# Attention and routing of a post-norm layer: one product for output and router logits, second variance on ScalarE, routing by eight tiles

## The chip, the cores and the metric

One Trainium2 chip; the kernel runs on one of its cores. The metric is the time of one execution on the device in microseconds (us), the median of several runs; the kernel before took 134.73 us (three runs, 134.23 to 137.53).

## What is computed

x is 2 x 1024 tokens of 128 floats. Weights: Wqkv 128 x 384, Wout 128 x 128, a router of 14 experts, and per expert w1 128 x 256 and w2 256 x 128 with biases. gamma and beta are not trivial.

```
xn  = layer_norm(x) * gamma + beta
q, k, v = split(xn @ Wqkv) in 16 heads of 8;  q = elu(q) + 1;  k = elu(k) + 1
kv  = sum over l of k v^T (per batch and head);  out = (q @ kv) / (q . sum(k) + 1e-6)
x   = layernorm(x + (x + out @ Wout))                # no gamma, no beta
logits = x @ router_w;  a = argmax(logits);  weight = softmax(logits)[a]
y   = (gelu(x @ w1[a] + b1[a]) @ w2[a] + b2[a]) * weight
return layernorm(x + y)
```

Everything is float32. Attention is linear: no token looks at another except through the sums kv and sum(k).

## The kernel before

The five engines run hand-written programs side by side, tied by semaphores; each engine works strictly in the order in which its calls stand. 2048 tokens are 16 tiles (NT) of 128; four tiles are a chunk c (C = 4), chunks 0 and 1 are batch 0, chunks 2 and 3 batch 1.

First part, attention and routing. Per chunk: VectorE (DVE) takes statistics of x (stats1), GpSimd (POOL) a power of -0.5 (rstd_1) and the normalized tiles (norm1, L341; chunk 0 on DVE, L526). TensorE (PE) transposes them (tr_x), ScalarE (ACT) copies them out with gamma and beta (xt, L392). TensorE makes q transposed (proj_q) and k, v (proj_kv); ACT takes exp and relu of q and k and copies v (L397 to L404), DVE joins them to elu + 1 (elu_q L545, elu_k L551). sum_kv adds the key-value sums and, by a column of ones in v_sb, sum(k) for a batch; heads (L557, L560) masks them into heads. num multiplies q with them, divide (L565 to L570) divides by the denominator, the result is transposed again (tr_att, at L408), multiplied with Wout (proj_out), and DVE adds 2 x (pre, L578), takes its statistics (stats2_, L582 to L587), POOL the power (rstd_2), DVE normalizes (x1, L593). These rows are transposed once more (tr_x1, x1t L412) and multiplied with the router (logits).

Routing, per chunk of four tiles: route (L603 to L610) finds the first largest logit in four dependent steps; eexp (L416) and weigh (L615, L616) make the weight, the 129th column of a row; store_x1 (L278, on SP's queue) writes the chunk's rows to DRAM. ranks adds, with matrices of ones, how many tokens go before each token when sorted by expert. After the last chunk: place (L621 to L629) and sixteen at_spot (L632) turn the ranks into one-hot matrices, invert multiplies them to the list of source rows, steps (L637 to L640) and step_row (L693) give the list of (tile, expert) pairs.

Second part, experts. All sorted tiles are gathered from DRAM by POOL (L365), which waits for the four stores and for sources (L644). 29 steps j (NP) follow, one pair of tile and expert each: SP copies the expert's w1 (L283), PE turns the tile (L905) and multiplies it, ACT applies gelu (L452), PE multiplies with w2, DVE adds (L710); finished tiles are normalized and scattered by POOL (L378). Each engine loads the list of experts into registers first. The orders of all engines around this change are the plain lists of calls at the end of each engine's function.

Of the kernel before, what the change touches and what calls it, by code (L numbers as in the profile page):

```python
# [17 lines left out]
I32 = mybir.dt.int32  # L18
# [22 lines left out]
TE = NT + 1  # L41
GROUPS = [(0, 1), (1, 4), (4, 8), (8, 12), (12, 15), (15, 16)]
# [19 lines left out]
def build(nc, x, gamma, beta, wqkv, wout, router_w, w1, b1, w2, b2, out):  # L62
    with ExitStack() as ctx:
# [29 lines left out]
        wout_sb = sb("wout_sb", [P, D])  # L93
        rw_sb = sb("rw_sb", [P, E])
        vec_rows = sb("vec_rows", [E * FC + 2, P])
# [12 lines left out]
        stats2 = sb("stats2", [P, NT, 6])  # L108
        mv2 = sb("mv2", [P, NT, 2])
        ve = sb("ve", [P, NT])  # L110
        ve2 = sb("ve2", [P, NT])
        rstd = sb("rstd", [P, NT])
        shift = sb("shift", [P, NT])
        rstd2 = sb("rstd2", [P, NT])
        exponent = sb("exponent", [P, C])
        xn = sb("xn", [P, NT, D])
        xn_t = sb("xn_t", [P, NT, P])
# [6 lines left out]
        v_sb = sb("v_sb", [P, NT, D + 1])  # L124
        kv_h = sb("kv_h", [P, B, D + H])
        den = sb("den", [P, C, H])
        rden = sb("rden", [P, C, H])
        att = sb("att", [P, NT, D])
        att_t = sb("att_t", [P, NT, P])
        pre = sb("pre", [P, NT, D])  # L130
        rows = sb("rows", [P, NT, ROW])
        x1_t = sb("x1_t", [P, NT, P])
# [3 lines left out]
        is_top = sb("is_top", [P, C, E])  # L136
        ranked = sb("ranked", [P, C, E])
# [3 lines left out]
        below = sb("below", [P, NT, E])  # L141
        e_exp = sb("e_exp", [P, NT, E])
# [31 lines left out]
        ps_t = ps("ps_t", [P, C, P])  # L174
        ps_q = ps("ps_q", [P, C * P])
        ps_kv = ps("ps_kv", [P, C, 2 * D])
        ps_acc = ps("ps_acc", [P, 512])
        ps_num = ps("ps_num", [P, 2, 512])
        ps_o = ps("ps_o", [P, C, P])
        ps_kvh = ps_acc[:, 0:D + 1]  # L180
        ps_vec = ps_acc[:, 0:E * FC + 2]
        num_v = ps_num[:, :, 0:2 * (D + H)].rearrange("p b (i n) -> p b i n", i=2)


        def ps_lg(c):
# [113 lines left out]
        def _(pool):  # L299
# [20 lines left out]
            for b in range(B):  # L320
                t = pool.iota(token_i[:, b * JB:(b + 1) * JB], pattern=[[1, JB]], base=b * S, channel_multiplier=JB)
# [636 lines left out]
```

## Time and profile before

| what | value |
|---|---|
| median of 3 runs | 134.73 us (134.23 to 137.53) |
| the profiled execution | 135.24 us |
| its span in the trace | 133.4 us |
| busy: PE, DVE, POOL, ACT | 86.3, 69.2, 54.4, 48.3 us |
| mean granted clock of TensorE | 0.833 |

The span runs from the first to the last recorded instruction; the rest of the 135.24 us lies round it. Engine names: PE is TensorE's matmuls, PEld its weight loads, SPq and ACTq the queues that issue DMAs. A float32 product of one tile is two rows (two weight loads and two matmuls) in the trace. L12 is line 12 of the kernel. The granted clock is 1.00 at 2.4 GHz and 0.50 at 1.2 GHz; in the first 12 us the rows say 1.00 although products there take as long as they do later at 0.50 (two rows of 512 columns 1.92 us from 11.25, and 1.02 us from 15.51).

### The profile page before, as it was taken

The numbers are of one execution on the slowest core, as the hardware profiler recorded it, in microseconds if no ns is written. First come the engines' busy times: TensorE is split into PE (matmuls) and PEld (weight loads), VectorE is DVE, ScalarE is ACT, GpSimd is POOL, SyncE is SP. The second block draws the span as 40 slices with busy tenths as digits, with TensorE's granted clock in tenths as the row PEclk, the third lists the DMA queues.
The fourth block names the chain that finished last, engine by engine and source line by source line (L and its number), as shares of the span: only waits on it lengthen the run. The fifth ranks groups of instructions, "written<-read, shape, count | busy, mean of one in ns | idle before, by whom it ended". The sixth has DMA issues, their size and how long they took to land.

```text
span 133.4 us, 2086 instructions
## 1 busy us (share of the span) xinstructions
PE 86.3 (65%) x547; PEld 71.3 (53%) x547; DVE 69.2 (52%) x297; ACT 48.3 (36%) x128; POOL 54.4 (41%) x78
## 2 busy tenths in 40 slices
PE   0038998989558953486370399989999886743000
PEld 0025686859457942366240399868788685632000
DVE  0999433688873897642793011433445766635000
ACT  1222786149210210120400144555556476553200
POOL 6386820004210003300005775757104386768871
PEclk9999999999968999655555557999999999995555
DMA  4899950000001002002200643455432433301110
GB/s 144 251 325 347 292 149 0 0 0 5 0 0 55 24 0 79 0 0 84 82 0 0 202 115 98 131 137 135 142 112 92 140 119 101 104 20 39 39 59 20
DMA packets 9673, 12.15 MB, mean 91 GB/s; under 512 B 1426, under 2 KB 7230, under 8 KB 9662
## 3 DMA queue, kind: packets, MB, share of 16 engines
q1 hardware_dynamic: 8420, 9.69, 22.4%
q0 software_dynamic: 1024, 2.11, 6.5%
q10 hardware_dynamic: 218, 0.22, 0.6%
q8 instruction: 5, 0.08, 0.3%
q14 instruction: 6, 0.05, 0.1%
HBM read 6.07 MB, written 2.11 MB: 61 GB/s over the span
## 4 chain that ended last, share of the span: by engine, by line
PE 38%; DVE 23%; POOL 18%; issue 8%; ACT 5%; DMA 2%; DVEq 1%; POOLq 1%
PE ps_kv L744 14%; POOL out L378 10%; PE ps_num L744 9%; POOL rstd L327 5%; PE ps_acc L744 4%; PE ps_q L744 3%; DVE rows L593 2%; DMA acc<-x_rows,source 2%; ACT k_parts L457 2%; DVE at_spot L632 2%; PE ps_o L792 2%; DVE pre L578 2%; DVE att L570 2%; PE ps_t L807 2%; DVE acc L710 1%
## 5 line engine op out<-in xcount | busy, mean ns | idle before, releaser
L327 POOL TENSOR_TENSOR rstd<-ve,exponent 128x4 f32<-128x4 f32 (+2 forms) x14 | 14.0, 999 | 42.4 <-DVE ve L587 32.0
L365 POOL DMA_INDIRECT acc<-x_rows,source x16 | 16.3, 1020 | 23.0 <-DVE source L644 16.8
L744 PE MATMUL ps_kv<-xs_t,w_cur 128*128 (+1 forms) x116 | 21.7, 316 | 1.7 <-DMA w_cur<-w_sb 1.2
L744 PE MATMUL ps_num<-w_sb,hid 128*128 x116 | 20.1, 299 | 3.7 <-ACT hid L452 3.2
L710 DVE SCALAR_TENSOR_TENSOR acc<-ps_num,share,acc 128x128 f32 (+1 forms) x29 | 10.2, 351 | 23.1 <-PE ps_num L744 18.9
L744 PEld LDWEIGHTS ps_kv<-xs_t,w_cur 128*128 128x128 f32 x116 | 16.8, 209 | 5.6 <-issue 4.6
L452 ACT ACTIVATE hid<-ps_kv,w_cur 128x128 f32<-128x128 f32 x58 | 18.1, 364 | 4.3 <-PE ps_kv L744 4.3
L378 POOL DMA_INDIRECT out<-k_parts,source x16 | 16.0, 999 | 7.9 <-ACT k_parts L457 5.7
L744 PEld LDWEIGHTS ps_num<-w_sb,hid 128*128 128x128 f32 x116 | 16.5, 205 | 5.1 <-issue 4.9
L457 ACT ACTIVATE k_parts<-acc,shift,rstd 128x128 f32<-128x128 f32 x16 | 7.1, 486 | 9.1 <-DVE shift L717 9.1
L744 PE MATMUL ps_kv<-wqkv_sb,xn_t 128*128 128x256 f32 x32 | 8.1, 396 | 0.4 <-ACT v_sb L404 0.4
L744 PEld LDWEIGHTS ps_kv<-wqkv_sb,xn_t 128*128 128x128 f32 x32 | 6.3, 204 | 2.9 <-ACT v_sb L404 1.2
L408 ACT COPY att_t<-ps_o 128x512 f32<-128x512 f32 x4 | 2.3, 586 | 14.0 <-PE ps_o L792 14.0
L807 PE MATMUL ps_t<-ident,rows 128*128 128x128 f32 x16 | 3.8, 377 | 5.6 <-DVE rows L593 5.6
L412 ACT COPY x_t<-ps_t 128x512 f32<-128x512 f32 x4 | 2.3, 585 | 13.8 <-PE ps_t L807 13.8
L447 ACT COPY xs_t<-ps_t 128x128 f32<-128x128 f32 x8 | 2.1, 266 | 14.0 <-PE ps_t L905 14.0
L744 PE MATMUL ps_num<-b_k,ones 128*128 x29 | 6.6, 229 | 0.0
L751 PE MATMUL ps_t<-ident,xn 128*128 128x128 f32 x16 | 3.4, 353 | 4.8 <-DVE xn L526 3.6
L341 POOL TENSOR_SCALAR xn<-x_sb,rstd,shift 128x128 f32<-128x128 f32 x12 | 5.7, 487 | 1.8 <-DVE shift L519 1.8
L807 PEld LDWEIGHTS ps_t<-ident,rows 128*128 128x128 f32 x16 | 2.5, 194 | 6.0 <-DVE rows L593 5.9
L392 ACT ACTIVATE xn_t<-ps_t,vec_cols 128x512 f32<-128x512 f32 x4 | 3.2, 790 | 6.5 <-PE ps_t L751 6.5
L744 PE MATMUL ps_num<-kv_h,q_t 128*128 128x144 f32 x32 | 4.8, 293 | 1.1 <-DVE kv_h L560 1.1
(123 smaller groups left out, 159.2 us busy)
## 6 DMA issues: line engine op xcount, KB each, us to landing
w_cur<-w_sb SPq DMA_DIRECT2D x29, 129.0 KB, 2.6
w_sb<-L_ffn_w SPq DMA_DIRECT2D x1, 1792.0 KB, 10.1
x_rows<-rows SPq DMA_DIRECT2D x4, 258.0 KB, 2.0
x_sb<-L_attn_x SPq DMA_DIRECT2D x4, 256.0 KB, 4.2
acc<-x_rows,source POOLq DMA_INDIRECT x16, 2.8
out<-k_parts,source POOLq DMA_INDIRECT x16, 2.3
wqkv_sb<-L_attn_Wqkv ACTq DMA_DIRECT2D x1, 192.0 KB, 4.9
wout_sb<-L_attn_Wout SPq DMA_DIRECT2D x1, 64.0 KB, 5.1
```

Source lines behind the costliest of these rows:

```text
L327: pool.tensor_tensor(out_, in_, exponent[:, 0:in_.shape[1]], ALU.pow).then_inc(done, 1)
L341: pool.tensor_scalar(xn[:, t, :], x_sb[:, t, :], rstd[:, t:t + 1], shift[:, t:t + 1], ALU.mult, ALU.add).then_inc(xn_ok, 1)
L365: pool.indirect_dma_start(acc[:, t, :], None, x1_rows, bass.IndirectOffsetOnAxis(ap=source[:, t:t + 1], axis=0), bounds_check=last_token, ...
L378: pool.indirect_dma_start(out_rows, bass.IndirectOffsetOnAxis(ap=source[:, t:t + 1], axis=0), res[:, t, :], None, bounds_check=last_token, ...
L392: act.activation(xn_t[:, C * c:C * c + C, :], ps_t[:], ACT.Identity, bias=vec_cols[:, E * FC + 1:E * FC + 2], scale=vec_cols[:, E * FC:E * ...
L452: act.activation(hid[:, k, c, :], ps_h[j % 2][:, c, :], ACT.Gelu, bias=w1_cur[:, k, F + c:F + c + 1]).then_inc(hid_ok, 1)
L457: act.activation(res[:, t, :], acc[:, t, 0:D], ACT.Identity, bias=shift3[:, t:t + 1], scale=rstd3[:, t:t + 1]).then_inc(y_ok, 1)
L570: dve.tensor_tensor(att[:, t:t + 2, :].rearrange("p i (h e) -> p i h e", e=HD), num_v[:, b, :, 0:D].rearrange("p i (h e) -> p i h e", e=HD ...
L710: dve.scalar_tensor_tensor(out=tile, in0=ps_y[j % 2], scalar=share[:].rearrange("p t e -> p (t e)")[:, bass.ds(tile_of(j, e) * E + e[j], 1 ...
L744: return pe.matmul(o, l, r, start=start, stop=stop)
L751: last = pe.transpose(ps_t[:, i, :], xn[:, C * c + i, :], ident[:])
L807: last = pe.transpose(ps_t[:, i, :], rows[:, C * c + i, 0:D], ident[:])
```

## The change

Output and logits from one product. The layer norm before the router takes off a mean and scales; both commute with the router's product. So Wout is multiplied on chip with [C | C Wr], where C = I - 1/128 centres and Wr is the router: cen_r, wo_t and wo_r (router_centre, weights_turn, weights_router, router_centred, router_out). The sums are now taken as v^T k (kv_t) and sum(k) in its own product with a column of ones (ps_ks), masked (own_heads) and multiplied with wo_r (values_out) into m_sb, 142 columns per batch. The queries are divided: den makes the denominators (epsilon comes in by a small product, den_eps), denominators takes the reciprocal, widen repeats it for the eight lanes of a head on ACT, turn_den transposes it, divide multiplies the transposed q. attend is then the one product; attended splits it into lg and pre (already centred up to 2 x). The part of the logits that comes from x itself is a product of the untouched transposed tiles (xh, residual) scaled by std (logits_x).

The second variance: squares on ACT, with the accumulated sum as output; POOL adds epsilon, takes the power and a shift (rstd_2); x1 is an ACT piece too. Logits are compared unscaled; soften scales them for the exponential once rstd2 is there.

Routing runs over eight tiles (p = 0, 1) instead of four (c = 0 to 3): route, eexp, weigh, ranks. Constants and the split of b2 move from DVE's head and middle: the iotas and the split to POOL behind norm1, the casts to DVE's middle. keep_busy adds products of zeros on TensorE (240 columns, bfloat16) at the start, behind the last attend, ranks(1) and invert, and ahead of the experts.

```diff
+            def residual(c):
+                for i in range(C):
+                    last = mm(res_of(c)[:, i, :], xh_t[:, C * c + i, :], cen_r[:, D:DL])
...
+                for t in range(C * c, C * c + C):
+                    mm(ps_kvt, v_sb[:, t, :], k_sb[:, t, :], False, False)
+                    last = mm(ps_ks, k_sb[:, t, :], one_col[:], False, t % JB == JB - 1)
...
+                mm(ps_m, kv_t[:, b, :], wo_r[:]).then_inc(m_ps, 1)
...
+                for i in range(C):
+                    last = mm(den_c[:, H * i:H * i + H], q_t[:, C * c + i, :], ks_h[:, c // CB, :], False, i == C - 1)
...
+                    last = pe.transpose(r_of(c)[:, i * P:i * P + P], q_exp[:, (C * c + i) * P:(C * c + i + 1) * P], ident[:])
...
+                for i in range(C):
+                    last = mm(ps_o[:, i, 0:DL], qs_t[:, C * c + i, :], m_sb[:, c // CB, :])
...
+            def squares(c):
+                act.wait_ge(pre_ok, c + 1)
+                act.wait_ge(neg2m_ok, 2)
+                for t in range(C * c, C * c + C):
+                    act.activation(rows[:, t, 0:D], pre[:, t, :], ACT.Square, bias=neg2m_s[:, t:t + 1], scale=ROOT_D,
+                                   accum_out=var2[:, t:t + 1]).then_inc(var2_ok, 1)
+            def x1(c):
+                act.wait_ge(shift2_ok, c + 1)
+                for t in range(C * c, C * c + C):
+                    act.activation(rows[:, t, 0:D], pre[:, t, :], ACT.Identity, bias=shift2[:, t:t + 1],
+                                   scale=rstd2[:, t:t + 1]).then_inc(x1_ok, 1)
...
+            def soften(p):
+                dve.wait_ge(rstd2_ok, CB * p + CB)
+                dve.tensor_tensor(scaled[:, o, :], below[:, o, :], rstd2[:, o].unsqueeze(2).to_broadcast([P, PT, E]),
+                                  ALU.mult).then_inc(below_ok, 1)
...
             def store_x1(c):
-                sp.wait_ge(x1_ok, c + 1)
-                sp.wait_ge(weight_ok, c + 1)
+                sp.wait_ge(x1_ok, C * c + C)
+                sp.wait_ge(weight_ok, c // CB + 1)
```

The lines of a diff are cut here; the order of TensorE's calls from the first sum on is now: sum_kv(1), residual(0), residual(1), values_out(0), den(0), den(1), proj_kv(2), residual(2), turn_den(0), residual(3), turn_den(1), proj_q(2), sum_kv(2), attend(0), proj_kv(3), attend(1), proj_q(3), sum_kv(3), values_out(1), den(2), den(3), ranks(0), turn_den(2), turn_den(3), attend(2), attend(3), 10 fillers, ranks(1), 14 fillers, invert, 4 fillers. DVE's from there: own_heads(0), elu_q(1), denominators(0), logits_x(0), logits_x(1), denominators(1), divide(0), logits_x(2), logits_x(3), divide(1), elu_k(2), constants, attended(0), elu_q(2), elu_k(3), attended(1), own_heads(1), elu_q(3), denominators(2), denominators(3), route(0), divide(2), divide(3), attended(2), attended(3), soften(0), route(1), place.

DVE between the one-hot matrices and the step list, before:

```order
L632 TENSOR_SCALAR at_spot<-col_no,spot 128x128 x16
L637 CAST begin_i<-ps_acc 128x14
L638 TENSOR_SCALAR btile_i<-begin_i 128x14 [waits dve_s]
L639 TENSOR_TENSOR begun<-btile_i,step_e 128x13 [waits dve_s]
L640 TENSOR_REDUCE count<-begun 128x1 [waits dve_s]
L644 CAST source<-ps_o 128x16 [waits src_ps]
L693 CAST step_row<-ps_t 1x32 [waits row_ps]
```

And after the change:

```order
L733 TENSOR_SCALAR at_spot<-col_no,spot 128x128 x16
L738 CAST begin_i<-ps_k 128x14
L739 TENSOR_SCALAR btile_i<-begin_i 128x14 [waits dve_s]
L740 TENSOR_TENSOR begun<-btile_i,step_e 128x13 [waits dve_s]
L741 TENSOR_REDUCE count<-begun 128x1 [waits dve_s]
L716 TENSOR_REDUCE e_sum<-e_exp 128x8 [waits eexp_ok]
L717 RECIPROCAL rows<-e_sum 128x8 [waits dve_s]
L710 TENSOR_TENSOR scaled<-below,rstd 128x112 [waits rstd2_ok]
L745 CAST source<-ps_a 128x16 [waits src_ps]
L716 TENSOR_REDUCE e_sum<-e_exp 128x8 [waits eexp_ok]
L717 RECIPROCAL rows<-e_sum 128x8 [waits dve_s]
L801 CAST step_row<-ps_t 1x32 [waits row_ps]
```

weigh(0), soften(1) (L710) and weigh(1) now stand round sources, behind at_spot; before, all weights were made ahead of place.

ACT's last work ahead of the Gelu table load, before:

```order
L408 COPY att_t<-ps_o 128x512 [waits at_ps]
L416 ACTIVATE e_exp<-below 128x56 [waits below_ok]
L408 COPY att_t<-ps_o 128x512 [waits at_ps]
L412 COPY x_t<-ps_t 128x512 [waits x1t_ps] x2
L416 ACTIVATE e_exp<-below 128x56 [waits below_ok] x2
L460 ACT_TABLE_LOAD
```

And after the change:

```order
L505 ACTIVATE rows,var<-pre,neg2m_s 128x128 [waits neg2m_ok,pre_ok]
L505 ACTIVATE rows,var<-pre,neg2m_s 128x128 x3
L511 ACTIVATE e_exp<-scaled 128x112 [waits below_ok]
L516 ACTIVATE rows<-pre,shift,rstd 128x128 [waits shift2_ok]
L516 ACTIVATE rows<-pre,shift,rstd 128x128 x3
L511 ACTIVATE e_exp<-scaled 128x112 [waits below_ok]
L516 ACTIVATE rows<-pre,shift,rstd 128x128 [waits shift2_ok]
L516 ACTIVATE rows<-pre,shift,rstd 128x128 x3
L516 ACTIVATE rows<-pre,shift,rstd 128x128 [waits shift2_ok]
L516 ACTIVATE rows<-pre,shift,rstd 128x128 x3
L574 ACT_TABLE_LOAD
```

The x1 pieces (L516) of chunks 2 and 3 stand behind the second e_exp; before, x1 was DVE's and stood ahead of its routing.

## Rows read from the trace of the kernel before

**Rows 1.** Stretches: width; busy PE, PEld, DVE, ACT, POOL; granted clock; DMA, GB/s
```profile
60.00:70.00 10.00, 5.95 (x39) 4.45 (x36) 6.64 (x35) 1.53 (x2) 0.00 (x0) 0.50 0.15 55
...
76.00:80.00 4.00, 4.00 (x19) 3.91 (x20) 0.39 (x2) 1.68 (x6) 3.09 (x4) 0.50 0.51 140
80.00:90.00 10.00, 9.50 (x68) 8.10 (x67) 3.25 (x13) 5.21 (x21) 6.46 (x7) 0.90 0.48 125
```

**Rows 2.** Timeline, handover from routing to experts: start us, us, instruction, [idle before <-releaser]
```profile
66.91 2.68 DVE L632 TENSOR_SCALAR at_spot<-col_no,spot 128x128 bf16<-128x128 bf16 x16
...
71.28 1.42 POOL L365 DMA_INDIRECT acc<-x_rows,source  x1 [16.80 <-DVE source L644]
73.00 1.00 POOL L365 DMA_INDIRECT acc<-x_rows,source  x1 [0.30 <-issue]
```

**Rows 3.** Timeline, start of the experts; last the store's DMA issues (KB, us to landing)
```profile
70.21 0.17 DVE L644 CAST source<-ps_o 128x16 int32<-128x16 f32 x1
...
73.16 6.68 SPq L283 DMA_DIRECT2D w_cur<-w_sb  x6
...
74.41 0.45 PE L905 MATMUL ps_t<-ident,acc 128*128 128x128 f32 x1 [3.80 <-DMA acc<-x_rows,source]
...
76.19 2.02 PE L744 MATMUL ps_kv<-xs_t,w_cur 128*128 128x128 f32 x8
...
x_rows<-rows SPq DMA_DIRECT2D x4, 258.0 KB, 2.0
```

**Rows 4.** Timeline, TensorE's products and transposes of four tiles
```profile
22.57 1.25 PE L744 MATMUL ps_num<-kv_h,q_t 128*128 128x144 f32 x8 [0.60 <-DVE kv_h L560]
...
29.99 1.89 PE L744 MATMUL ps_kv<-wqkv_sb,xn_t 128*128 128x256 f32 x8
...
32.61 1.06 PE L744 MATMUL ps_acc<-v_sb,k_sb 128*128 128x129 f32 x8
...
33.58 0.66 PE L807 MATMUL ps_t<-ident,rows 128*128 128x128 f32 x4
...
34.96 1.03 PE L744 MATMUL ps_q<-rw_sb,x_t 128*128 128x14 f32 x8 [0.72 <-issue]
...
55.97 1.89 PE L744 MATMUL ps_q<-rw_sb,x_t 128*128 128x14 f32 x8 [0.68 <-ACT x_t L412]
```

**Rows 5.** Timeline and groups by form: pieces of ACT, DVE and POOL
```profile
8.50 1.79 POOL L341 TENSOR_SCALAR xn<-x_sb,rstd,shift 128x128 f32<-128x128 f32 x4 [0.39 <-DVE shift L519]
...
19.42 0.59 ACT L403 ACTIVATE k_parts<-ps_kv 128x512 f32<-128x512 f32 x1
...
19.89 0.59 ACT L404 COPY v_sb<-ps_kv 128x512 f32<-128x512 f32 x1
...
51.13 0.69 DVE L578 SCALAR_TENSOR_TENSOR pre<-x_sb,ps_o 128x512 f32<-128x512 f32 x1 [0.80 <-PE ps_o L744]
...
53.25 1.11 DVE L593 TENSOR_SCALAR rows<-pre,mv,rstd 128x128 f32<-128x128 f32 x4
...
58.40 0.22 DVE L605 TENSOR_TENSOR ranked<-is_top,prio 128x56 f32<-128x56 f32 x1
...
64.97 0.39 DVE L621 TENSOR_TENSOR place_m<-ps_acc,chosen 128x224 f32<-128x224 f32 x1 [0.41 <-PE ps_acc L744]
...
122.59 1.26 ACT L457 ACTIVATE k_parts<-acc,shift,rstd 128x128 f32<-128x128 f32 x3 [2.07 <-DVE shift L717]
...
125.69 0.49 ACT L457 ACTIVATE k_parts<-acc,shift,rstd 128x128 f32<-128x128 f32 x1 [1.83 <-DVE shift L717]
...
L327 POOL TENSOR_TENSOR rstd<-ve,exponent 128x4 f32<-128x4 f32 x8 | 9.0, 1119 | 34.6 <-DVE ve L587 32.0 <-DVE ve L513 2.6
...
L567 DVE RECIPROCAL rden<-den 128x64 f32<-128x64 f32 x4 | 2.2, 553 | 0.1
```

**Rows 6.** Stretches of one us where the clock falls, columns as in rows 1
```profile
36.00:37.00 1.00, 0.00 (x0) 0.00 (x0) 0.23 (x1) 0.00 (x0) 1.00 (x1) 1.00 0.00 0
...
38.00:39.00 1.00, 0.69 (x3) 0.70 (x4) 0.90 (x5) 0.00 (x0) 0.00 (x0) 0.50 0.00 0
```

More of the change, by code:

```diff
@@ new lines, in eexp @@
+            def eexp(p):
+                o = slice(PT * p, PT * p + PT)
+                act.wait_ge(below_ok, p + 1)
+                act.activation(e_exp[:, o, :], scaled[:, o, :], ACT.Exp).then_inc(eexp_ok, 1)
+            def x1(c):
[3 more added lines that the diff above has]
+                                   scale=rstd2[:, t:t + 1]).then_inc(x1_ok, 1)
@@ L433, in _ @@
-            kv(3)
-            x1t(0)
-            x1t(1)
+            xh(3)
+            heads_out(0)
+            widen(0)
+            widen(1)
+            k(2)
+            v(2)
+            q(2)
+            k(3)
+            v(3)
+            q(3)
+            heads_out(1)
+            widen(2)
+            widen(3)
+            squares(0)
+            squares(1)
+            x1(0)
+            squares(2)
+            squares(3)
             eexp(0)
-            at(2)
+            x1(1)
@@ L843, in invert, with keep_busy @@
                 last.then_inc(src_ps, 1)
+            def keep_busy(bank, n):
+                for i in range(n):
+                    mm(bank, ones[:], nothing[:])
+            idle_k = ps_k[:, 2, 0:240]
+            idle_q = ps_q[:, 0:240]
+            pe.wait_ge(filler_ok, 2)
+            keep_busy(idle_k, 16)
             pe.wait_ge(pool_c, P_IDENT)
@@ L875, in _ @@
-            logits(0)
-            tr_x1(1)
+            sum_kv(1)
+            residual(0)
+            residual(1)
+            values_out(0)
+            den(0)
+            den(1)
+            proj_kv(2)
+            residual(2)
+            turn_den(0)
+            residual(3)
+            turn_den(1)
+            proj_q(2)
+            sum_kv(2)
+            attend(0)
+            proj_kv(3)
+            attend(1)
+            proj_q(3)
             sum_kv(3)
-            num(2)
-            pe.wait_ge(pool_c, P_ONES)
@@ L880, in _ @@
-            pe.wait_ge(consts_ok, N_CONSTS)
+            values_out(1)
+            den(2)
+            den(3)
             ranks(0)
-            logits(1)
-            tr_att(2)
-            num(3)
-            proj_out(2)
-            ranks(1)
-            tr_att(3)
-            proj_out(3)
-            tr_x1(2)
-            logits(2)
-            tr_x1(3)
-            ranks(2)
-            logits(3)
-            ranks(3)
+            turn_den(2)
+            turn_den(3)
+            attend(2)
```

641 lines of the change are left out of this document (361 added, 280 removed).

## The prediction

> About 2% (2.7 us) is what a measurement of this kernel can tell from no change.
>
> **What bounds it now.** I read the stretches first. From 60 to 70 us TensorE is busy for 5.95 of 10 us at a granted clock of 0.50, its 1.2 GHz level, and it is still there from 76 to 80; the mean of 0.90 from 80 to 90 puts the rise at 82 [rows 1]. So there are two parts. Until about 70 us each engine waits for another in turn and none is full. After the routing the experts run on TensorE, and at the end POOL's queue of scatters. Then the handover between the two: the sixteen at_spot end at 69.59, POOL begins the first gather at 71.28 and takes 1.3 for each further one [rows 2]; the source indices leave DVE at 70.38, TensorE turns the first gathered tile at 74.41 and has the first expert from 76.19 [rows 3], 6.6 us behind at_spot. Nothing behind that point is edited except for filler products, so the change pays as far as this start comes earlier, or the clock there is higher.
>
> **Durations.** In float32 a product of four tiles with 14 columns takes 1.03 us at full clock and 1.89 at half [rows 4]: only the weight loads count, 0.24 a tile at full clock. With 256 columns it takes 1.89, with 144 columns 1.25, with 129 columns 1.06, and four transposes 0.66 [rows 4]. Some 0.16 to 0.2 of each is the way out of the array, which the next product covers, so they occupy TensorE for 1.71, 0.96, 0.9 and 0.43. Two ACT pieces of 512 columns begin 0.5 apart, a reciprocal of 64 takes 0.55, an element-wise DVE step of 512 takes 0.69 [rows 5]. A link of the routing chain is 0.22 us at 56 elements [rows 5]; at DVE's 0.69 for 512, 56 more add 0.07, so 0.3 at 112 with its wait.
>
> **The first part, laid out with these.** It ends at 69.6 now. After the change:
> 1. The constants leave DVE's head and the shift before the second normalization goes, so POOL's norm(1), at 8.50 now [rows 5], begins about 7.7 and takes 1.8. With TensorE kept warm by 32 filler products, one set of transposes 0.43 and the first key/value product 1.9 bring it to 11.8. Cold it would be about 2 more.
> 2. ACT's exp, relu, v and the new copy xh, 4 x 0.5, let tr_x(2) go at 14.0; 0.43 and 1.9: the second key/value product ends at 16.3.
> 3. ACT again, 3.1 us for k(1), v(1), xh(1), q(0); then q(1) 0.85 and transposes 0.43 on TensorE. sum_kv now loads two sets of weights a tile, 8 x 0.24 = 1.9 against 0.9: 22.7. Here the kernel stands at 22.57 now, with its first num product [rows 4]: the xh copies and the longer sums have eaten the early lead.
> 4. TensorE in its order: residual 4 x 0.94, values_out 0.24, den 2 x 1.0, key/value(2) 1.71, turn_den 2 x 0.43, q(2) 0.85. That is 9.4, to 32.1.
> 5. elu_k(2) stands behind divide(1): 0.7; sum_kv(2) 1.9; attend(0) 0.95; key/value(3) 1.7; ACT 1.1; elu_k(3) 0.7; sum_kv(3) 2.0; masks 0.5; den(2), den(3) 2.4; reciprocal 0.6; 0.5 for handovers: 44.6 + 0.5 = 45.1.
> 6. route(0) over eight tiles 4 x 0.3 + 0.5 = 1.7; ranks(0), 3304 columns at 2.4 GHz, 1.4; a turn 0.6; divide 0.7; attend(2) 1.1; lg and pre 0.9; attend(3) 1.1; lg and pre 0.9; 0.3 for handovers: 53.8. soften(0) 0.3, route(1) 1.7, ranks(1) 1.2; place from place_m to at_spot 1.95 and at_spot 2.65 as now [rows 2, 5]: 61.7.
>
> That is 7.9 us before the 69.6 of now. Gone are the transposes of att and x1, their copies, proj_out and the logits as products of their own, of which the last rounds ran at half clock, two of four routing chains, and the statistics of pre on DVE. The same layout made for the kernel of now comes to 71.1, so it is more likely long than short where the clock is high.
>
> **What it gives back.** The rows of the two orders show a new chain. The x1 pieces of chunks 2 and 3 stand on ACT behind eexp(1), which needs soften(1), and that stands on DVE behind at_spot, steps and weigh(0). POOL gathers only when all four stores have landed. From 61.7: steps 0.8, weigh(0) 0.5, soften(1) 0.3, eexp 0.35, then eight x1 pieces. One ACT piece of this form takes 0.49 and three take 1.26 [rows 5], so 0.39 each: 3.2, to 66.9. The last store needs 2.0 from issue to landing [rows 3]: 69.0; POOL's 0.9, as between 70.38 and 71.28: the first gather at 69.9. Now x1 is long done and the gather stands 1.7 behind at_spot; then 8.2. Of 7.9 us, 6.5 are given back. With the distances of now turn(0) comes 3.1 later, at 73.0, and the first expert at 74.8 instead of 76.2: 1.4 earlier. SP's first weight copy, issued at 73.16 [rows 3], 2.8 behind the sources, now stands behind the last store: 67.3 + 2.8 = 70.1. That is 4.7 ahead of the first expert, 3.0 before: hidden. weigh(1), behind sources, is done by 64.2, under x1. Behind the x1 pieces on ACT is only the Gelu table load, which ends before turn(0).
>
> DVE does four x1 pieces in 1.11 us [rows 5], 0.26 each with its tail off, where ACT needs 0.39. The Trainium skill, "ScalarE: Activation LUTs" (Rules for kernel authors), puts plain multiplies and adds on VectorE and not on ScalarE, and so speaks against this move; by it the eight late pieces would take 2.1 instead of 3.2. The trace agrees on which engine is faster, though in float32 by a factor of 1.5 only. The sum goes by the order as written, 3.2.
>
> Operations without a row. Squares with an accumulated output: from 0.26 (DVE's piece) to 0.8 (an ACT piece and as much again for the read-out), I take 0.4; chunk 3's squares and POOL's power (mean 1.12 [rows 5]) end by 57, soften(1) asks at 63.0, so a cover of 6 us makes both ends cost nothing. The widening copy: 0.4 to 1.0, taken as 0.5 by the copies of 512; from den(3) to turn_den(2) it is partly hidden by route(0), so 0 to 0.5 more. Products with one column: 0.24 a tile by the row with 14 columns, bounds 0.12 and 0.3; sixteen on the path, -2 to +1. The split of b2 and the constants on POOL lie in its idle time between 17 and 47.
>
> **The clock.** TensorE had nothing to do from 36 to 37 at a granted clock of 1.00, and had 0.50 from 38 to 39 [rows 6]. After the change idle stretches of 2.5 us (44.4 to 46.9) and 2.1 us (53.8 to 55.9) remain; a short fall in one of them costs about 0.5, which I add. At the experts' start the clock is 0.50 from 76.2 to 82 now [rows 1]: at full clock that work takes 2.9 less, of which the gathers, 1.3 apart [rows 2], let perhaps 2.2 through. 24 fillers now run from about 66.7 and 6 between the first turns, but 3 to 4 us without work lie between. Held warm it is -2.2, cold 0; I take 1.1.
>
> The Trainium skill, "TensorE: Matmul & The Clock Gate" (HAM oscillation), warns that waits between bursts put the array back to half rate. If that acts between these fillers and turn(0), this term is 0 and the sum 1.1 higher; the fall at 38 shows that it can.
>
> Sum: span 133.4 - 1.4 - 1.1 + 0.5 = 131.4. The profiled execution took 135.24, 1.84 round its span, so 133.2 after; it stands 0.5 above the median of 134.73, which gives 132.7.
>
> **Rivals.**
> A. The clock holds: fillers carry it to the experts, no gap drops it, and the layout is a microsecond long as it was for now: 133.4 - 1.4 - 2.2 - 1.0 = 128.8, by the median 130.1. For it: fillers stand ahead of every late wait. Against: the gap ahead of turn(0).
> B. Slower: the clock falls while ranks(0) waits for route(0) and stays at half until the routing is done, as it does from 55 to 70 now. The products from 47 to 57 double (ranks, turns, attend): +3.3, and the experts start cold: 133.4 - 1.4 + 3.3 = 135.3, by the median 136.6. It decides from where at_spot ends later than 63.1, since only 1.4 are left after the give-back. With the fall at 42, under den, it is +6.9: 140.2.
> C. The late stores are no wait, something lets x1(3) go early: 7.9 and the clock's 1.1 come through, 125.7. The orders of DVE and ACT speak against it.
>
> Forecast 0.45, A 0.27, C 0.03, B 0.25. Faster by over 2% (under 132.0): A, C and a sixth of the forecast, 0.37. Slower by over 2% (over 137.4): the heavy part of B, 0.15. Within: 0.48. Range 129.3 to 137.0.
>
> **What would show it.** At_spot ends between 60 and 63; eexp(1), eight ACT pieces of 0.39 and the last store lie between it and the first gather, which begins 8 us behind it; the first expert at 74.8. The granted clock at 77 tells A from the rest. It is wrong if the gather stands less than 6 us behind at_spot, or at_spot ends after 64.

## The result, and the profile after

The changed kernel took 142.64 us in the median of four runs (140.84 to 145.81) beside 136.13 (134.23 to 137.78) of the kernel before: ratio 1.052, 95% interval 1.041 to 1.064. It is slower; the prediction was 132.7, range 129.3 to 137.0. Every kernel also has executions some per cent slower than its fastest, so each ratio here is taken between the faster executions of both kernels, while the times given are medians of all. The profiled execution is the 145.81 one, 3 us above the median, with the lowest mean clock of the four (0.821); so its times are read for where the excess lies, and the median for how large it is. Its span is 144.1 us.

The stretches of the changed kernel. Columns as in rows 1; the last three rows answer to those of [rows 1]:

```profile
20.00:30.00 10.00, 8.90 (x64) 8.25 (x64) 2.54 (x5) 6.63 (x13) 5.31 (x20) 0.89 0.02 4
30.00:40.00 10.00, 10.00 (x42) 9.29 (x43) 2.12 (x6) 2.80 (x5) 0.00 (x0) 0.50 0.00 1
40.00:50.00 10.00, 10.00 (x42) 8.58 (x42) 3.57 (x13) 1.08 (x2) 0.00 (x0) 0.59 0.00 0
...
60.00:70.00 10.00, 8.21 (x51) 6.91 (x51) 3.92 (x12) 6.22 (x29) 3.87 (x8) 0.74 0.00 1
...
76.00:80.00 4.00, 2.31 (x17) 1.28 (x16) 3.52 (x22) 1.30 (x4) 0.00 (x0) 0.87 0.14 51
80.00:90.00 10.00, 5.76 (x37) 4.26 (x37) 0.54 (x2) 4.03 (x10) 4.38 (x5) 0.71 0.49 158
```

From 30 to 40 us TensorE has work in every microsecond and a granted clock of 0.50, its 1.2 GHz level. In [rows 1] the low clock went with 5.95 busy us of ten; from 76 to 80 us TensorE was busy throughout at 0.50 there too, but the clock had been low since 55 us, behind three microseconds (51 to 54) almost without work. Here it falls under work. Single microseconds of the same trace show the fall:

```profile
26.00:27.00 1.00, 1.00 (x12) 1.00 (x11) 0.61 (x3) 0.50 (x2) 0.00 (x0) 1.00 0.00 0
27.00:28.00 1.00, 1.00 (x10) 1.00 (x10) 0.42 (x1) 0.00 (x0) 0.00 (x0) 0.87 0.02 4
28.00:29.00 1.00, 1.00 (x6) 0.92 (x6) 0.00 (x0) 0.00 (x0) 0.00 (x0) 0.50 0.03 5
```

What TensorE does there, in the timeline: the sixteen records of residual(0) and (1), two dens of four tiles, then the key/value product of four tiles that takes 3.76 us instead of the 1.89 of [rows 4].

```profile
26.21 2.19 PE L852 MATMUL ps_o<-cen_r,xh_t 128*128 128x14 f32 x16
...
28.93 1.87 PE L852 MATMUL ps_r<-ks_h,q_t 128*128 128x16 f32 x8
...
32.37 3.76 PE L852 MATMUL ps_k<-wqkv_sb,xn_t 128*128 128x256 f32 x8
```

At the start, the product of router weights waits for its load, six fillers stand behind it, and only then come the first transposes. These run at half speed, and the first key/value product does for a part (1.06 us for four transposes, 2.55 for the product; 0.63 and 1.89 later on), although 28 fillers had gone before the first transposes:

```profile
8.47 0.58 PE L852 MATMUL ps_o<-rw_sb,cen_r 128*128 128x14 f32 x2 [2.25 <-DMA rw_sb<-L_ffn_router_w]
8.89 1.36 PE L852 MATMUL ps_k<-nothing,ones 128*128 128x240 bf16 x6
10.04 1.06 PE L863 MATMUL ps_t<-ident,xn 128*128 128x128 f32 x4
...
12.76 2.55 PE L852 MATMUL ps_k<-wqkv_sb,xn_t 128*128 128x256 f32 x8
```

The chain of waits of the same kernel goes through POOL: its pieces, its small constants, and only then the first key/value sum (ps_a).

```profile
7.82 3.14 POOL xn L360 x4
...
16.48 3.68 POOL xn L360 x4
...
20.92 0.03 POOL one_col L406
20.95 0.15 POOL before L407
21.10 2.04 PE ps_a L852 x17
```

And the handover, in the timelines of DVE, ACT, POOL and TensorE, which answers to [rows 2, 3]:

```profile
74.73 2.69 DVE L733 TENSOR_SCALAR at_spot<-col_no,spot 128x128 bf16<-128x128 bf16 x16
...
78.90 3.17 ACT L516 ACTIVATE rows<-pre,shift,rstd 128x128 f32<-128x128 f32 x8
...
84.41 1.30 POOL L430 DMA_INDIRECT acc<-x_rows,source  x1 [11.44 <-DMA x_rows<-rows]
...
89.20 0.62 PE L852 MATMUL ps_q<-xs_t,w_cur 128*128 128x128 f32 x4
```

At_spot ends at 77.4 (69.6 before, 61.7 predicted). The first gather stands 7.0 behind it (1.7 before), the first expert 4.8 behind the gather, and the last scatter begins 51.0 us behind the first expert (140.15 - 89.20) where it was 53.4.

### The profile page after: what moved, and what is told of

It is laid out like the page before. It is cut to its first block, busy times and chain, and to the rows that moved or that the text cites. A ratio compares the mean times of both kernels' runs of the same rounds, so it can differ in the third digit from the quotient of the medians.

```text
span 144.1 us, 2336 instructions
## 1 busy us (share of the span) xinstructions
PE 108.0 (75%) x666; PEld 90.1 (63%) x666; DVE 54.9 (38%) x224; ACT 61.4 (43%) x178; POOL 64.8 (45%) x99
## 4 chain that ended last, share of the span: by engine, by line
PE 43%; POOL 22%; DVE 14%; issue 6%; DMA 5%; ACT 5%; DVEq 1%; POOLq 1%
PE ps_o L852 12%; PE ps_k L852 10%; POOL out L443 9%; PE ps_a L852 7%; POOL xn L360 7%; PE ps_q L852 6%; POOL rstd L349 5%; PE ps_t L852 2%; PE ps_r L852 2%; ACT rows L516 2%; DMA acc<-x_rows,source 2%; DMA x_sb<-L_attn_x 2%; ACT k_parts L571 2%; DVE at_spot L733 2%; DMA x_rows<-rows 1%
## 5 line engine op out<-in xcount | busy, mean ns | idle before, releaser
L852 PE MATMUL ps_o<-w_sb,hid 128*128 x116 | 19.2, 290 | 3.4 <-ACT hid L566 3.4
L852 PEld LDWEIGHTS ps_o<-w_sb,hid 128*128 128x128 f32 x116 | 15.6, 196 | 4.4 <-issue 4.1
L818 DVE SCALAR_TENSOR_TENSOR acc<-ps_o,share,acc 128x128 f32 (+1 forms) x29 | 10.2, 351 | 21.0 <-PE ps_o L852 14.3
L852 PE MATMUL ps_q<-xs_t,w_cur 128*128 (+1 forms) x60 | 10.4, 297 | 1.7 <-DMA w_cur<-w_sb 1.4
L566 ACT ACTIVATE hid<-ps_q,w_cur 128x128 f32<-128x128 f32 x30 | 9.3, 364 | 2.4 <-PE ps_q L852 2.4
L360 POOL TENSOR_SCALAR xn<-x_sb,mv,rstd 128x128 f32<-128x128 f32 x12 | 9.9, 839 | 0.6 <-POOL rstd L349 0.6
L852 PE MATMUL ps_k<-wqkv_sb,xn_t 128*128 128x256 f32 x32 | 10.2, 475 | 0.0
L852 PE MATMUL ps_k<-xs_t,w_cur 128*128 x56 | 9.8, 297 | 0.4
L566 ACT ACTIVATE hid<-ps_k,w_cur 128x128 f32<-128x128 f32 x28 | 8.7, 365 | 1.7 <-PE ps_k L852 1.7
L852 PE MATMUL ps_a<-k_sb,v_sb 128*128 128x128 f32 x32 | 8.4, 357 | 0.1
L483 ACT ACTIVATE k_parts<-ps_k 128x512 f32<-128x512 f32 x4 | 2.4, 597 | 12.7 <-PE ps_k L852 12.7
```

The source lines that it names most:

```text
L360: pool.tensor_scalar(xn[:, t, :], x_sb[:, t, :], mv[:, t, 0:1], rstd[:, t:t + 1], ALU.subtract, ALU.mult).then_inc(xn_ok, 1)
L483: act.activation(k_exp[:, o, :], ps_k[:, :, 0:D], ACT.Exp).then_inc(k_act, 1)
L566: act.activation(hid[:, k, c, :], ps_h[j % 2][:, c, :], ACT.Gelu, bias=w1_cur[:, k, F + c:F + c + 1]).then_inc(hid_ok, 1)
L818: dve.scalar_tensor_tensor(out=tile, in0=ps_y[j % 2], scalar=share[:].rearrange("p t e -> p (t e)")[:, bass.ds(tile_of(j, e) * E + e[j], 1 ...
L852: return pe.matmul(o, l, r, start=start, stop=stop)
```

## The experiments

Sixteen kernels ran in four groups of four, each group on a chip of its own, so a time is compared only with the kernel before of its own group. In the first group (n_shift, n_contig, s_order, c_wide) that took 140.79 us, 4 to 6 more than in the others, and in all four traces ACT waits once for 2.4 to 3.5 us, 2 to 4 us behind the first expert, for something that the profile doesn't name; from the first gather to the last scatter they need 62.6 to 64.2 us, where all other traces need 55.7 to 58.4. No run tried why. These four are therefore read up to the first gather.

**1 and 2. POOL's pieces.** n_shift:

```diff
-  pool.tensor_scalar(xn[t], x_sb[t], mv[t, 0], rstd[t], ALU.subtract, ALU.mult)
+  pool.tensor_scalar(xn[t], x_sb[t], rstd[t], shift[t], ALU.mult, ALU.add)   # shift = -mean * rstd on DVE
```

> The changed kernel with one edit: POOL's norm1 in the form of before, x times rstd plus shift, the shift again made by DVE. Theory: the new form (x minus mean, times rstd) is what took POOL 3.12 us for four pieces instead of 1.79, and three such chunks stand on the path of the start (rows 7.82, 12.16, 16.48). Then four pieces take 1.8 again, sum_kv(0) begins at about 17 instead of 21.1, and the time falls by about 4 us to 138 or 139. Rival: POOL is slow because of what DVE or the DMAs do beside it, then four pieces stay at 3 us and the time stays at 142 to 143.

n_contig keeps subtract and mult, but takes the mean from a dense copy:

```diff
+  dve.tensor_copy(mean[chunk], mv[chunk, 0])
-  pool.tensor_scalar(xn[t], x_sb[t], mv[t, 0], rstd[t], ALU.subtract, ALU.mult)
+  pool.tensor_scalar(xn[t], x_sb[t], mean[t], rstd[t], ALU.subtract, ALU.mult)
```

> The changed kernel, norm1 still subtract then multiply, but the mean is read from a tile of its own, one number beside the next (a DVE copy), instead of every second number of mv. If the pair of operations is what POOL is slow at, four pieces stay at 3.1 us. If it is the place of the mean, they go back to 1.8 us.

n_shift took 151.51 us (147.12 to 152.43) beside 140.79, where 138 or 139 was expected, and n_contig 149.98 in its one run; no run tells why n_shift is this slow at its end. The dense mean left a piece at 0.79 us; multiply and add brought it to 0.45, as in the timeline of n_shift (four pieces):

```profile
8.27 1.74 POOL L361 TENSOR_SCALAR xn<-x_sb,rstd,shift 128x128 f32<-128x128 f32 x4 [0.38 <-DVE shift L643]
```

So the pair of operations sets the price. The sums of chunk 0 began at 18.9 instead of 21.1. The first batch's sums, DVE's kv_t(0), came at 27.4 us: no earlier than the 26.5 of the changed kernel's first trace, but that trace had no fall of the clock near 22 us, and n_shift has one. Its neighbours on the same chip, which have it too and keep the dear pieces (n_contig and s_order), come at 29.7 and 29.6. So the price was worth some 2 us there, by way of the column of ones behind the pieces (run 15), and 0.9 to 1.3 us at the end of at_spot (73.8, beside 74.7 and 75.1).

**3. Order of the handover.** s_order:

```diff
 ACT:  x1(1)  -eexp(1)  x1(2)  x1(3)  +eexp(1)
 DVE:  place  -at_spot  -steps  weigh(0)  soften(1)  +at_spot  +weigh(1)  +steps  sources  -weigh(1)
```

(at_spot is the end of place in the changed kernel.)

> The changed kernel with another order alone: on ACT x1(2) and x1(3) ahead of eexp(1); on DVE weigh(0) and soften(1) between the ids and the at_spot, weigh(1) ahead of steps and sources. Theory of the late stores: the first gather then begins 2 to 3 us behind the last at_spot instead of 7.0, though at_spot itself comes up to 1 us later; the time falls by 4 us. Rival: the experts' start is set by something else (SP's weight copies, register loads, fillers), then it falls by less than 1.5 us.

145.42 us, ratio 1.017 (1.001 to 1.034). Its ACT and POOL timelines:

```profile
68.43 4.71 ACT L516 ACTIVATE rows<-pre,shift,rstd 128x128 f32<-128x128 f32 x12
73.05 0.28 ACT L511 ACTIVATE e_exp<-scaled 128x112 f32<-128x112 f32 x1
...
78.62 1.30 POOL L430 DMA_INDIRECT acc<-x_rows,source  x1 [8.50 <-DMA x_rows<-rows]
```

The x1 pieces now lie under the search for the places. The gather stands 3.5 behind at_spot instead of 7.0 (2 to 3 was expected). The give-back of the prediction existed, and half of it was only order.

**4, 5 and 6. Wide products among the narrow ones.** A filler is a bf16 product of 240 columns, as the changed kernel has them elsewhere. c_wide:

```diff
 residual, den:  for i in range(C):
                     mm(14 or 16 columns)
+                    mm(filler)
```

> The changed kernel with one product of zeros of 240 columns behind each tile of residual and den (32 more in all, 0.1 us each at full clock). Theory: the granted clock falls to 0.50 at 28 and at 55 us, with TensorE busy all the time, because the products there have 14 or 16 columns and do little but load weights; with wide products among them it stays at 1.00, the stretch from 26 to 48 us shrinks by 6 to 9 us less 1.6 for the new products, and the time falls by 4 to 7 us. Rival: the clock falls for another reason (its own time grid, the load of earlier work), then the record is as before and the time grows by 1.6 to 3 us.

c_block sets the same fillers as four in a row ahead of each group of four; c_res has them in the residual alone.

> The changed kernel with the same 32 filler products of 240 columns as in the run that set one behind each narrow product, but in blocks of four ahead of each residual and each den, so that the narrow products still stand four in a row. Theory (the clock falls under runs of products that stream few columns for the time they occupy TensorE, and one wide product between two of them prevents it): the fall near 28 us comes again or only some us later, and most of 30 to 45 us is at 0.50. Rival (any extra wide products in that stretch hold the clock): 1.00 from 20 to 50 us, as with the interleaved ones, and at_spot ends at 66 to 68 us.

> The changed kernel with a wide filler behind each narrow product of the residual alone; den stays as it is (14 or 16 columns, four in a row). Theory: nothing falls at 28 us, since the residual's products no longer stand alone; den(0) and den(1) follow at 29 to 32 us and are the next narrow run, so the fall comes there, 2 to 5 us later, and at_spot ends between 67 and 76 us. Rival (the residual alone is the cause): 1.00 until 50 us, at_spot at 67 us.

Stretches of c_wide, of c_block and of c_res, in this order:

```profile
20.00:30.00 10.00, 9.22 (x87) 8.61 (x88) 3.15 (x8) 6.33 (x14) 4.99 (x19) 1.00 0.02 4
30.00:40.00 10.00, 9.54 (x77) 8.49 (x76) 4.01 (x17) 3.86 (x7) 0.00 (x0) 1.00 0.00 1
```

```profile
20.00:30.00 10.00, 8.93 (x62) 7.75 (x62) 2.53 (x5) 5.38 (x11) 4.81 (x18) 0.83 0.01 4
30.00:40.00 10.00, 9.54 (x76) 8.36 (x77) 3.91 (x14) 3.79 (x8) 0.00 (x0) 1.00 0.00 1
```

```profile
20.00:30.00 10.00, 9.03 (x41) 7.89 (x42) 0.92 (x3) 4.72 (x9) 4.40 (x19) 0.60 0.02 4
30.00:40.00 10.00, 10.00 (x50) 9.47 (x50) 2.25 (x7) 1.51 (x3) 0.00 (x0) 0.50 0.00 0
```

At_spot ends at 66.8 in c_wide, 71.6 in c_block, 78.2 in c_res. In c_block the rival was right as far as the clock goes: it had a short fall from 22 to 25, before the residual, and then held to 53, so four narrow products in a row did no harm here with four wide ones ahead of them; at_spot came later than the rival's 66 to 68. In c_res neither came: its clock fell at 22 us, before the residual, behind 2.7 us without work, and did not rise until 42, although the residual had its fillers by then. So there are two falls. The one at 28 stands alone in the changed kernel's first trace, and c_wide is its control: both wait 1.19 us ahead of the first sums, neither falls at 22, and with the fillers step 4 of the prediction takes 9.9 us (25.9 to 35.8) instead of 16.4. c_wide took 144.46 us, ratio 1.034 (1.021 to 1.047), where 4 to 7 us less was expected: of the 8 us by which its at_spot is earlier than n_contig's and s_order's on the same chip (10.6 earlier than in the first trace) the end shows little, on the chip with the unnamed wait. c_block took 140.62 us and c_res 147.28, one run each, beside 135.76.

**7, 8 and 9. Controls on another chip.** The changed kernel and the kernel before, unedited; and b_sub, the kernel before with the changed kernel's pair of operations:

```diff
-  pool.tensor_scalar(xn[t], x_sb[t], rstd[t], shift[t], ALU.mult, ALU.add)
+  pool.tensor_scalar(xn[t], x_sb[t], mv[t, 0], rstd[t], ALU.subtract, ALU.mult)
```

> The changed kernel, unedited, run beside the next three on one chip so that they can be compared with it. Theory (two mis-sized terms: POOL's pieces at 0.79 us instead of 0.45, and the clock at half under the narrow products): as in the first profile, the second set of key/value sums starts near 21 us, the clock is 0.50 for most of 30 to 45 us with TensorE busy throughout, at_spot ends at 75 to 78 us and the first gather stands 7 us behind it. Ratio to the kernel before 1.04 to 1.07. Rival (the chip of the first runs was the cause): at_spot ends before 70 us here and the ratio is under 1.03. The wait of 2.4 to 3.5 us of ACT for an unseen releaser behind the first expert, which the four variants so far all show and the first profile of the changed kernel does not: if it comes from the edits it is absent here, if it comes from the execution it can be here too.

> The kernel before, unedited, with a profile taken on the same chip. Theory: at_spot ends near 69.6 us and the first gather begins near 71.3 us, as in the first profile; if there is more in its time than then, it lies behind the first gather (until the last scatter 58.3 us then), as ACT's wait of 2.4 to 3.5 us and a lower clock. Rival: this chip is slower in the part up to the routing, so that at_spot ends after 72 us.

> The kernel before with one edit: POOL's twelve normalized tiles as (x - mean) * rstd, the form of the changed kernel, in place of x * rstd + shift. Theory (the pair of operations sets the price): one piece takes 0.79 us instead of 0.45, a chunk 3.1 us instead of 1.8, the three chunks +4 us in sum, and at_spot ends 2 to 4 us later, since chunks 1 to 3 gate the key/value products in turn. Rival (the price comes from what else runs beside it in the changed kernel, ACT's or DVE's traffic): the pieces keep 0.45 us.

The changed kernel: 140.74 us beside 135.12, ratio 1.038 (1.029 to 1.046), at_spot to 76.4, gather 7.0 behind, no unnamed wait. Its clock falls at 22 us, behind a wait of 2.68 us for the column of ones, rises at 29 and falls again at 32.4, with work in every microsecond, to 46. The kernel before (137.15 us in this run): at_spot to 72.1, 2.5 later than in its first trace (its mean clock from 40 to 50 us was 0.69), and 57.7 us from the first gather to the last scatter; so its excess over the first trace lies ahead of the gather, as the rival had it, and one trace against another carries some 2 us of this kind. B_sub's first chunk on POOL:

```profile
8.51 3.22 POOL L341 TENSOR_SCALAR xn<-x_sb,mv,rstd 128x128 f32<-128x128 f32 x4 [0.39 <-DVE shift L519]
```

0.80 a piece: the price is the pair's alone, as the theory had it. Its first sums come 1.3 us late and the second batch's 1.4 us late, yet at_spot ends at 71.7, no later than in the unedited kernel of this chip, and the time is 137.48 us beside its 137.15 (one run each). 2 to 4 us was expected; 1.4 came and was lost again, where the unedited kernel's clock was low for longer (39 to 46 us; b_sub's 40 to 43).

**10. Three repairs at once.** all3 is n_shift, s_order and c_wide together.

> The changed kernel with all three repairs: the normalization as x * rstd + shift (POOL 0.45 us a piece), eexp(1) and the late x1 pieces set ahead of at_spot, steps and sources, and a wide filler product of 240 columns behind each narrow one of the residual and of den. Theory (the three causes add): POOL's part takes 3 to 4 us from at_spot, the clock 8 to 10 us, so at_spot ends at 62 to 66 us and the first gather stands 3.5 us behind it, at 66 to 69 us, against 71.3 in the kernel before: ratio 0.95 to 0.99. Rival (the give-back moves on: the experts then begin cold or wait for weights): the first gather is as early but the time is within 1% of the kernel before.

134.12 us beside 135.12, ratio 0.997 (0.993 to 1.000): 4.7% under the unedited changed kernel's 140.74 on the same chip. At_spot ends at 66.8, as in c_wide, though the pieces are cheap here (its clock falls from 22 to 25 us, c_wide's did not). The gather stands 3.5 behind it, at 70.3. Expected were 62 to 66, 66 to 69 and a ratio of 0.95 to 0.99; what came is nearer to the rival. Two stretches offer a reason. The 24 fillers ahead of turn(0):

```profile
71.35 4.96 PE L865 MATMUL ps_q<-nothing,ones 128*128 128x240 bf16 x24 [3.13 <-issue]
```

run at half clock and hold the first gathered tile, issued at 70.3, until 76.1; in the changed kernel they began at 82.95, ahead of the first gather, and its 3 us covered most of them. And at the start:

```profile
8.20 0.38 PE L865 MATMUL ps_o<-rw_sb,cen_r 128*128 128x14 f32 x2 [1.96 <-DMA rw_sb<-L_ffn_router_w]
...
9.57 1.06 PE L876 MATMUL ps_t<-ident,xn 128*128 128x128 f32 x4
```

the product of router weights waits for its load, with six fillers behind it, ahead of the first transposes, whose input is ready at 7.5.

**11 and 12. Those two.** all3_rc sets the router product behind the first transposes; all4 has 4 fillers instead of 24 as well.

```diff
-  router_centre(); keep_busy(6); tr_x(0)
+  keep_busy(6); tr_x(0); router_centre()
...
-  keep_busy(idle_q, 24)
+  keep_busy(idle_q, 4)
```

> The kernel with the three repairs, with a fourth: the product of router weights, which waits for its load until 8.2 to 8.5 us, and the six fillers behind it no longer stand ahead of the first transposes in TensorE's order; the product comes behind them. Theory (this wait, which the prediction left out, is most of the 2.2 us by which the first key/value product ends late): the first transposes begin near 7.6 us instead of 9.6, the first key/value product ends at 12 to 12.5 instead of 14, at_spot ends 1 to 2 us earlier than the 66.8 of three repairs; ratio 0.98 to 0.99 to the kernel before. Rival (ACT's exits or POOL's pieces bind right behind it): kv_t(0) moves by less than 0.5 us and the ratio stays at 0.997.

> The same with a fifth edit: 4 fillers instead of 24 ahead of the first gathered tile's turn. In the run with three repairs these 24 ran at half clock, 4.96 us from 71.35, and held turn(0) until 76.3 us, though the first gathered tile had landed near 74. Theory: turn(0) begins when its tile lands, 4 us behind the first gather, so the first expert starts about 2 us earlier than in the run before this; of that 1 to 2 us reach the end, ratio 0.965 to 0.985. Rival (the fillers pay for themselves in clock: without them the experts begin at half clock, as in the kernel before): the first expert is earlier, the clock is 0.50 for its first 4 to 6 us and the ratio is that of the run before this or worse.

134.86 us (130.61 to 135.03) and 132.71 (129.26 to 134.81) beside 135.76; no interval, and the two overlap. In all3_rc the first key/value product ends at 12.3 instead of 13.8, but kv_t(0) comes at 27.8 and at_spot ends at 67.8, each a microsecond later than in all3, where 1 to 2 earlier was expected: TensorE was done earlier, then waited 2.14 us for the column of ones, and its clock was at 0.50 from 20 to 26 (in all3 from 22 to 25). The clock ate the lead. In all4 the first expert begins at 76.5, 1.8 earlier than in all3_rc, as expected, at half clock for its first microsecond.

**13 and 14. Narrowness by itself.** In the kernel before, behind the first batch's sums, where TensorE waits for nothing:

```diff
+  b_narrow: for i in range(32): mm(unused, xn_t[i % 4], wqkv_sb[:, 0:14])
+  b_broad:  for i in range(16): mm(unused, xn_t[i % 4], wqkv_sb[:, 128:384])
```

> The kernel before with 32 float32 products of 14 columns (what the residual and den are made of) set on TensorE behind the first batch's key/value sum, where its granted clock is 1.00 and it waits for nothing; their results are not used. Each occupies 0.24 us, 7.7 us in all, with TensorE busy throughout. Theory (a run of narrow products is itself enough to lower the clock): it falls to 0.50 within or right behind the block, between 25 and 32 us, although TensorE is busy 1.00 of each us; later steps move by 8 us or more. Rival (the falls come from idle stretches alone): the clock stays 1.00 through the block, as long as TensorE is busy.

> The control to the run before: the same place and the same 7.5 us, filled with 16 float32 products of 256 columns, 0.47 us each. Both theories: the clock stays at 1.00 through the block. If it falls here too, it is not the narrowness but the length of the busy stretch, and the theory of the narrow products is wrong.

Stretches of b_narrow, then of b_broad:

```profile
26.00:27.00 1.00, 1.00 (x11) 1.00 (x11) 0.00 (x0) 0.00 (x0) 0.00 (x0) 1.00 0.00 0
27.00:28.00 1.00, 1.00 (x8) 1.00 (x7) 0.00 (x0) 0.00 (x0) 0.00 (x0) 0.64 0.00 0
28.00:29.00 1.00, 1.00 (x7) 1.00 (x6) 0.00 (x0) 0.00 (x0) 0.00 (x0) 0.50 0.00 0
```

```profile
26.00:27.00 1.00, 1.00 (x6) 0.87 (x6) 0.00 (x0) 0.00 (x0) 0.00 (x0) 1.00 0.00 0
27.00:28.00 1.00, 1.00 (x7) 0.87 (x6) 0.00 (x0) 0.00 (x0) 0.00 (x0) 1.00 0.00 0
28.00:29.00 1.00, 1.00 (x6) 0.90 (x5) 0.00 (x0) 0.00 (x0) 0.00 (x0) 1.00 0.06 16
```

Both are busy in every microsecond of their blocks (21.8 to 30.2 and 23.0 to 30.0). Under the narrow products the clock falls at 27.3, stays at 0.50 behind them to 34, and the 1.89 us product there takes 2.79; under the broad ones it never moves. So narrow products are enough for a fall, without a wait. The times do not tell the two apart: 143.56 us for b_narrow, 145.61 for b_broad, one run each beside 137.04, since b_broad's clock falls later, at 43 us in a wait, and stays low to 57. And one thing is left of the changed kernel's own fall: in its first trace only 1.5 us of the residual had gone by, with the sums ahead of it (per tile one product of 128 columns and one of a single column). c_wide left these as they were and held; how much they add, no run parts.

**15. The column of ones.** a_one writes it ahead of POOL's normalizations:

```diff
+  pool.memset(one_col[:], 1.0)
   norm1(1); norm1(2); norm1(3); spreads()
-  pool.memset(one_col[:], 1.0)
```

> The changed kernel with the column of ones that the key/value sums multiply by written on POOL before its normalizations, not behind them; nothing else. In the changed kernel TensorE waits at 19.9 to 21.1 us for POOL's row of constants behind the twelve pieces. Theory (the sums wait for this column, not for the pieces of their own chunk, so that it, and not the pieces' price, is what gives the late first part): the sums of chunk 0 run at 18 us while ACT reads chunk 1, q(1) begins near 21 and kv_t(0) comes at 24 to 26 us instead of 26.5 to 30; the idle stretch before q(1) stays, so the clock still falls once near 20 and again under the narrow products; time 0 to 2% below the unedited changed kernel. Rival (the pieces of chunk 2 and 3 bind): kv_t(0) moves by less than 0.5 us.

140.65 us, ratio 1.047 (1.035 to 1.059), no gain that can be told. The sums of chunk 0 now run at 18.3 instead of 21.1. But q(1) waits for ACT as before:

```profile
21.64 1.45 PE L852 MATMUL ps_q<-xn_t,wqkv_sb 128*128 128x512 f32 x2 [1.44 <-ACT q_pos L478]
```

and the clock falls at 22 behind that gap, so kv_t(0) comes at 26.7 (24 to 26 was expected): earlier than in the second trace of the unedited kernel (29.9), not than in the first (26.5), where no fall came at 22. ACT sets q(1) in the first trace as well: it begins 3.23 us behind the second key/value product there, here and in all6. So the column by itself cost nothing in the first trace; in the second it made the wait of 2.68 us, behind which the clock fell. This trace, of a 140.28 us execution, shows the second fall too:

```profile
28.00:29.00 1.00, 1.00 (x11) 0.98 (x10) 0.00 (x0) 0.28 (x1) 0.00 (x0) 1.00 0.02 4
29.00:30.00 1.00, 1.00 (x8) 1.00 (x8) 0.09 (x1) 0.00 (x0) 0.00 (x0) 0.54 0.00 0
30.00:35.00 5.00, 5.00 (x17) 4.28 (x18) 1.21 (x4) 1.23 (x2) 0.00 (x0) 0.50 0.00 0
```

**16. All of it.** all6 is all4 with a_one's edit and with 12 fillers behind the sums of chunk 0.

```diff
   sum_kv(0)
+  keep_busy(a free bank, 12)
   proj_q(1)
```

> The kernel with the five edits (normalization as multiply and add, x1 ahead of at_spot, wide fillers between the narrow products, router product behind the first transposes, 4 fillers at the experts), and with the column of ones early and 12 wide fillers behind the sums of chunk 0, where TensorE idled and the clock fell to 0.50 from 19.8 to 26.7 us. Theory: 1.00 from 10 to 50 us, kv_t(0) at 23 to 24.5 us instead of 27.8 to 28.1, at_spot ends 3 to 4 us earlier than the 68 of then, at 64 to 65; ratio 0.94 to 0.965 to the kernel before. Rival (DVE or the late stores take it back): the first gather moves by less than 2 us from 71.6 us.

130.92 us (130.66 to 132.47) beside 137.04, ratio 0.976 (0.963 to 0.988), above the expected 0.94 to 0.965: it is faster than the kernel before, though whether by over 2% is not clear, and a_one, the changed kernel but for one column, took 140.65 on the same chip. The clock is 1.00 from 10 to 48 us, kv_t(0) comes at 24.0, at_spot ends at 65.5, the gather begins at 69.05. Two falls are left: one from 65 to 75 us, round the handover, and one in front of ranks(0), behind 2.1 us without work (stretch of all6):

```profile
48.00:50.00 2.00, 1.76 (x11) 1.51 (x12) 0.33 (x2) 2.00 (x12) 1.03 (x2) 0.53 0.01 4
```

## Why the prediction was wrong, by its steps

**Steps 1 to 3 (22.7 us): measured 26.4, +3.7.** Of this, 3.3 us are there at once: the first key/value product ends at 15.1, not 11.8. The prediction left out the wait for the router's weights and took TensorE as "kept warm by 32 filler products", where the first transposes and a part of this product ran at half speed. In all6, with the router product behind the transposes, the ones early and the gap filled, the product ends at 12.6 and the sums at 23.7, one microsecond from the forecast. The piece on POOL was mis-sized as well (a chunk 3.1, not 1.8). It delays the column of ones, which the prediction put among the constants that "lie in its idle time": one of them had a reader. That cost nothing in the first trace and a fall of the clock in the second.

**Step 4 ("that is 9.4, to 32.1"): measured 16.4, from 26.4 to 42.7, +6.9.** This is the step that failed. Each term was taken at full clock from [rows 4], and the clock was questioned only where TensorE would idle. It fell with the engine full, under products of 14 to 16 columns, as it does in b_narrow under nothing but such products, and what followed took twice as long. With fillers among them the step takes 9.9, in c_wide (25.9 to 35.8) and in all6 (23.7 to 33.6).

**Steps 5 and 6 (29.6 us): measured 34.7, +5.1.** The same low clock to 48, and again from 55, begun under den(2), to 65, the wait of ranks(0) included. In all3, where the clock stays at 1.00 until 66 us, it is 30.4 (36.4 to 66.8), so 0.8 of the 5 is the layout's own, and that with weigh(0) and soften(1) ahead of at_spot. In all6, with the fall ahead of ranks(0), it is 31.9.

**What it gives back (8.2 us between at_spot and gather): measured 7.0**, by the chain that the prediction named, with eight pieces in 3.17 (3.2 predicted) and 2.0 for the store. The pieces began 0.5 sooner behind at_spot than laid out, and POOL 0.3 behind the last store's landing instead of 0.9. The first expert was to come 4.9 behind the gather and came 4.8 behind. This part held.

**The clock at the experts.** It was 1.00 when they began, so the prediction's best case (-2.2) came: 2.4 less from first expert to last scatter, against the 14.4 us by which the first expert came later than forecast.

**The sum.** 3.7 + 6.9 + 5.1 is 15.7 at at_spot; the handover gave 1.3 back (first expert at 89.2, forecast 74.8), and what stands behind the first expert took 1.7 less than forecast, so the span is 12.7 above the 131.4. At the median the excess is 9.9. How long the clock stays low differs: in the six traces without fillers among the narrow products the fall with TensorE busy comes at 28 to 32 us and lasts 7 to 20 us, 20 in the first trace, which is of the slowest run. In a_one's, of a 140.28 us execution, it lasts from 29.1 to 35.9, and a like one, begun under den(2) and den(3), from 49.6 to 59.8. The three parts are then 26.5, 12.4 and 32.8 us, over the forecast by 3.8, 3.0 and 3.2, and at_spot ends at 71.7. There the same step fails by less than half as much, and the start weighs as much as it.

**Rivals.** B was slower and priced at 136.6 to 140.2, with a fall "at 42, under den", but told it as a fall in a wait. A rested on fillers ahead of every late wait; none stands ahead of the wait of ranks(0) (2.24 us in the first trace), and it says nothing on narrow work. The chance of 0.15 for slower came from counting idle gaps alone. The Trainium skill, "TensorE: Matmul & The Clock Gate" (HAM oscillation), warns of waits between bursts: the traces agree for the falls at 22 us (2.68 us without work in the second trace) and at 48 us (2.13 in all6). Under b_narrow's block there was no such wait.

## What to carry to other kernels

A product with few columns costs its weight load (1.03 us for four tiles of 14 columns, 1.06 with 129 [rows 4]), and a run of them can cost the clock of what follows: look at the granted clock where TensorE is full, not only where it waits. If such products must be, a wide filler behind each is nearly free: with one the narrow products of the residual stand 0.25 us apart in all3, without one 0.22 in a_one. A lead won at an engine's front can come back as an idle gap that drops the clock, so a repair there can need the next one to be worth something (all3_rc and all4, then all6); and of every constant that is moved behind other work, ask who reads it first.

## What the runs showed of the hardware

- TensorE at a granted clock of 1.00, with work in each microsecond, fell to 0.50 within a block of float32 products of 14 columns (from 21.8; the fall at 27.3 us), and did not fall in a block of products of 256 columns at the same place (one trace of each).
- A POOL piece of 128x128 float32 takes 0.79 to 0.80 us as subtract and multiply with two columns of operands, and 0.45 as multiply and add, in both kernels; in the changed one it stays at 0.79 when the mean lies dense.
- The kernel before took 135 to 137 us in the median beside the first result and in three groups, and 140.8 in the fourth. There ACT's wait of 2.4 to 3.5 us without a named releaser stood in all four traces. Its cause is open; no run of the kernel before was profiled there.
- The changed kernel's clock falls at 22 us in its second trace, behind 2.68 us without work, and not in its first, behind 1.19. In n_shift, a_one and all3 it falls at 22 to 23 us, behind 1.44.
- Still open: why ahead of ranks(0) the same wait of 2.13 us is followed by a fall in c_wide and all6 and by none in all3, and why a fall under narrow products lasts 7 us in one trace and 20 in another.
